# The attention sum of a graph layer: the next group's values weighed ahead of this group's one-hots

## The reference, cut to what matters

```python
q = (feat @ Wq.T + bq).reshape(n, H, HD)          # H = 8 heads of HD = 32
k = (feat @ Wk.T + bk).reshape(n, H, HD)
v = (feat @ Wv.T + bv).reshape(n, H, HD)
score = jnp.einsum('ehd,ehd->eh', q[edge_dst], k[edge_src])
score = jnp.clip(score / math.sqrt(HD), -10.0, 10.0)
...
ex = jnp.exp(score - smax[edge_dst])
den = jax.ops.segment_sum(ex, edge_dst, num_segments=n)
alpha = ex / den[edge_dst]
wv = jax.ops.segment_sum(alpha[:, :, None] * v[edge_src], edge_dst, num_segments=n).reshape(n, C)
```

## Time and profile before

| what | value |
|---|---|
| median of 3 runs | 4137.75 us (4130.2 to 4140.1) |
| the profiled execution's own time | 4135.46 us |
| its span (first to last instruction) | 4133.7 us |
| busy over the span: PE, DVE, ACT, POOL | 63%, 53%, 30%, 32% |
| attention sum, first product to last gather's landing | 2444 to 3240 us |

### The profile page before, as it was taken

How to read it: one execution, slowest core, us unless ns; L and a number is a source line. 1 busy time by engine, 2 the same in 40 slices (tenths; PEclk the granted TensorE clock), 3 DMA queues, 4 the chain that set the end, 5 groups by cost and what they waited for, 6 DMA issues and landing times. The chain is left out here.

```text
span 4133.7 us, 66642 instructions
## 1 busy us (share of the span) xinstructions
PE 2615.2 (63%) x17072; PEld 2109.2 (51%) x17073; DVE 2172.5 (53%) x4422; ACT 1260.5 (30%) x2441; POOL 1312.0 (32%) x996
## 2 busy tenths in 40 slices
PE   3513334437587799975654426666766487699993
PEld 2413333324276577753444325445545466589983
DVE  5623323231555488883347736666666655544443
ACT  0200000003244155551477512222222244244440
POOL 0038888842000000000001136667767500510015
PEclk9955555557688699987777658999888778799996
DMA  2036566730000000002000046666665100356643
GB/s 116 23 93 161 144 170 159 193 86 6 0 21 0 15 15 15 15 8 100 14 1 0 0 120 159 159 163 168 168 165 161 54 21 0 126 177 231 232 162 85
DMA packets 263746, 383.33 MB, mean 93 GB/s; under 512 B 122411, under 2 KB 189607, under 8 KB 258810
## 3 DMA queue, kind: packets, MB, share of 16 engines
q0 software_dynamic: 156960, 171.31, 16.8%
q1 hardware_dynamic: 93850, 199.08, 14.5%
q10 hardware_dynamic: 12864, 12.06, 1.0%
HBM read 318.81 MB, written 62.55 MB: 92 GB/s over the span
## 5 line engine op out<-in xcount | busy, mean ns | idle before, releaser
L1685 POOL DMA_INDIRECT as_gkv<-gather_kv,as_index x415 | 565.7, 1363 | 280.5 <-DVE as_index L1836 170.5
L745 POOL DMA_INDIRECT ms_got<-gather,ms_index x400 | 505.9, 1265 | 128.6 <-issue 109.3
L812 PE MATMUL ms_total<-ms_got,ms_hot 125*125 125x256 f16 x1040 | 231.7, 411 | 382.8 <-DMA ms_got<-gather,ms_index 292.9
L812 PEld LDWEIGHTS ms_total<-ms_got,ms_hot 125*125 x1040 | 203.6, 219 | 411.1 <-issue 411.1
L1806 PE MATMUL as_total<-as_gkv,as_hot 125*125 125x264 f32 x1040 | 280.0, 420 | 76.1 <-DVE as_summed L552 66.1
L2093 POOL MEMSET bm_fx<- 128x128 f32 x1 | 0.2, 204 | 1012.9 <-POOLq L114 1012.9
L1806 PEld LDWEIGHTS as_total<-as_gkv,as_hot 125*125 125x125 f32 x1040 | 201.2, 202 | 127.6 <-issue 91.4
L1479 ACT ACTIVATE ex_h<-ex_up,ex_now 128x313 f32<-128x313 f32 (+1 forms) x320 | 195.8, 612 | 197.6 <-PE ex_up L457 190.4
L2749 DVE CAST moe_hidden<-moe_h 128x256 f16<-128x256 f32 (+1 forms) x336 | 107.3, 319 | 206.2 <-ACT moe_h L2696 206.2
L1818 DVE TENSOR_TENSOR z_flat<-as_picked,as_gkv 125x1280 f32<-125x1280 f32 x81 | 120.4, 1487 | 176.7 <-DMA as_gkv<-gather_kv,as_index 130.2
L2696 ACT ACTIVATE moe_h<-moe_up,moe_w 128x256 f32<-128x256 f32 (+1 forms) x336 | 163.2, 486 | 140.3 <-PE moe_up L457 95.4
(11 more groups left out here) (431 smaller groups left out, 5859.1 us busy)
## 6 DMA issues: line engine op xcount, KB each, us to landing
moe_w<-wsplit SPq DMA_DIRECT2D x34, 2052.0 KB
as_dsts<-in_dst SPq DMA_DIRECT2D x83, 305.2 KB
wsplit<-ms_split SPq DMA_DIRECT2D x36, 512.0 KB, 4.3
pairs<-z_flat SPq DMA_DIRECT2D x4, 2048.0 KB, 21.5
ms_raw<-in_L_ffn_W1p SPq DMA_DIRECT2D x16, 512.0 KB, 6.9
ms_raw<-in_L_ffn_W2p SPq DMA_DIRECT2D x16, 512.0 KB, 9.2
moe_rows<-pairs SPq DMA_DIRECT2D x32, 256.0 KB
results<-moe_made SPq DMA_DIRECT2D x32, 256.0 KB, 8.2
```

Source lines behind the costliest of these rows:

```text
L745: pool.indirect_dma_start(out=got[:, s, j, :], out_offset=None, in_=m.gather0, in_offset=bass.IndirectOffsetOnAxis(ap=index[:, s, j:j + 1] ...
L812: ins = pe.matmul(total[:, visit % RING, 0:C], hot[:, visit % RING, j, :], got[:, s, j, p * C:(p + 1) * C], start=(j + p == 0), stop=(j + ...
L1685: pool.indirect_dma_start(out=gkv[:, s, j, 0:2 * C], out_offset=None, in_=m.gather_kv, in_offset=bass.IndirectOffsetOnAxis(ap=index[:, s, ...
```

## The change

In each of the four bodies, `weigh(n + 1)` moves from behind the loop of visits to the place between `next_index` and that loop. No instruction is added, removed or changed in shape, and no semaphore has another count.

```diff
                         next_index(n + SLOTS - 1, (s - 1) % SLOTS)
+                        weigh(n + 1, (s + 1) % SLOTS)
                         with dve.Fori(0, count) as k:
...
                             adder.add(visit, tile)
-                        weigh(n + 1, (s + 1) % SLOTS)
                 v.leave(G // SLOTS)
```

## The result

The changed kernel takes 4176.19 us, the median of 4 runs (4168.31 to 4177.7); the kernel before, run beside it, 4138.93 (4130.2 to 4141.86). The ratio is 1.009, 95% interval 1.007 to 1.011: **about 37 us slower**. That is 18 us beyond the upper end of the range. The profiled execution took 4177.7 us, 42.2 more than the one of before, with a span of 4176.0.

What follows compares the result with a forecast made beforehand. It took the bound to be a ring: a double body plus a two-body gather round. Double bodies +4.8, clock −2 and gathers −2 summed to +0.8 us, giving a forecast of 4138.5 us, range 4120 to 4158.

Steps and rivals of the forecast that it cites:

- The one-hots come later: On DVE, the one-hots start 1.50 us behind the index copy instead of 0.76, which is 0.74 later.
- Double bodies: Bodies with two visits: +0.1 us each, +0.5 at a trip's end, as the sequencer's table reading comes into the open; +4.8 us.
- Rival C: Double bodies take the whole 0.74 us delay, nothing won back behind the second visit: +18 us, 4156; chance 10%.
- The gathers' issue: POOL's gathers, held by DVE instructions with two SBUF inputs: 1.01 us a round instead of 1.08, −0.1 each, −2 in all.
- Rival D: Multiplication and one-hots back to back hold a round's first and fifth gathers 0.8 us longer: +38 us, 4176; chance 5%.
- Rival A: DVE's loop is the bound, so the covered idle ahead of the one-hots counts: −36 us, 4102; chance 5%.
- The lap: Stage's repeating unit: a double body plus a two-body gather round of 18.2 us from its end; shorter single bodies buy nothing.
- TensorE's clock: PE's first sums in double bodies, starting later, leave part of the low-clock stretch behind: −2 us, bounds −5 to +5.
- where the stretch ends when it did: Clock assumption: with the low-clock stretch's end fixed, a sum 0.74 us later leaves up to 0.37 us of it behind.
- the gathers' landing: Gather start to landing, called worst known: a shifted transfer of destinations could move it half a us either way, ±12 us.
- rival E: The gathers land later, mirror of a rival with sooner landings: +19 us, 4157; chance 7%.
- The signs: Checks in DVE's waits: waits for gathers grow by some 20 us; the wait for the first sum falls some us under 80.4.

Runs made afterwards that it cites:

- e9: Kernel before, with the wait for the last sum and the index copy moved between product and sum by head in each body: 4081.16 us, ratio 0.9873.
- e5: Kernel before, plus two matmuls of zeros into an unused bank between PE's picks and sum in every body: 4146.76 us, ratio 1.0011.
- e6: Changed kernel, plus two matmuls of zeros into an unused bank between PE's picks and sum: 4152.81 us, ratio 1.0029 to the kernel before.
- e1: Kernel before, with the transfers of destinations cut to 5 of 125 partitions from the third group on: 4103.43 us, ratio 0.9905.
- e2: Changed kernel, with the transfers of destinations cut to 5 of 125 partitions from the third group on: 4115.78 us, ratio 0.9931 to the kernel before.
- e3: Kernel before, with each full transfer of destinations issued later, waiting also for the next body's product: 4143.83 us, ratio 1.0002.
- e4: Changed kernel, with each full transfer of destinations issued later, waiting also for the next body's product: 4156.56 us, ratio 1.0037 to the kernel before.
- e8: Changed kernel, with destinations' transfers cut to 5 of 125 partitions and two matmuls of zeros between picks and sum: 4099.99 us, ratio 0.9904 to the kernel before.
- e7: Kernel before, with two memsets into an unused bank behind the index copy, delaying the one-hots without the move: 4177.45 us, ratio 1.008.

## Why the prediction was wrong

**Right.** *The one-hots come later*: 1.52 for 1.50 behind the index. *Double bodies*, the sequencer's part: behind the second one-hots the sequencer reads the table and reaches its last wait at 3058.9,

```profile
L523 DVEq TENSOR_LOAD <-group_table x1: 311/311/311, 3058.2 to 3058.2; - x1
```

```profile
L1817 DVEq EVENT_SEMAPHORE  x1: 21/21/21, 3058.9 to 3058.9; - x1
```

1.6 behind one-hots of 3057.28 (forecast 1.7), and the product starts 1.70 behind them (1.85). Where TensorE had its full clock through the body, a double body that is the first or second of its trip is 10.62 to 10.64 us long after and was 10.73: 0.1 shorter, not 0.1 longer. In the third place it is 10.84 (10.71 to 10.74 before), and in the last 11.15 to 11.16 (10.66 in two of four before), 0.5 longer as forecast for a trip's end. On average over all 24 bodies the one-hots' 0.74 costs 0.12 us, since 0.62 comes back behind the second ones: +3 in all, where +4.8 was forecast. Rival C, for which the product had to stay 2.53 behind, falls. *The gathers' issue*: the first gather of a round, the second and the one that meets the next body's multiplication,

```profile
3063.52 1.58 POOL L1685 DMA_INDIRECT as_gkv<-gather_kv,as_index  x1 [5.25 <-DVE as_index L1836]
3065.40 1.21 POOL L1685 DMA_INDIRECT as_gkv<-gather_kv,as_index  x1 [0.30 <-issue]
...
3069.97 1.69 POOL L1685 DMA_INDIRECT as_gkv<-gather_kv,as_index  x1 [0.30 <-issue]
```

took 1.58, 1.21 and 1.69; 1.57 and 1.21 were forecast for the first two, and for the last 1.21 + 0.65, 0.17 too much. The issue of the five took 8.03 us on average, 8.12 before: −0.09, and −0.1 was forecast. **Rival D had the number of the result, 4176, and is refuted all the same**: the first gathers of the 24 rounds took 1.57 to 1.59 us, nowhere near 2.2. The Trainium skill (SBUF — State Buffer, SBUF: two separate sides) infers that a two-input multiplication leaves descriptor generation alone; as in the earlier trace rows, the 1.58 us contradict it. Rival A falls, since the gather waits took up all that the single bodies lost, and more. *The lap*: held by e9.

**Wrong, first term: TensorE's clock.** I took −2 with −5 to +5 as bounds. The step that failed is "where the stretch ends when it did": I moved the sum 0.74 us along a stretch of low clock whose end I held fixed, or moved by as much. I did not ask what fills the 0.74. In most bodies of before there was no gap to fill, since the sum followed the picks; now PE pauses 0.77 there, right after the long pause of the gather wait. The stretch of low clock at the double body was 3.4 or 6.8 us long in 23 of the 24 laps of before; now it is 10.2 or 13.7 in 16 of them. The first sum grew from 3.06 to 3.64 on average, +0.58 × 24 = +14, which is what the wait for it shows (80.4 to 94.4). The other part of the body's +0.90 is ahead of the one-hots, which start 5.12 into the body where it was 4.19: +0.93, and not +0.74, since in four bodies (3, 22, 51, 70) the index itself waited for PE's last sum, +4.9 us in all; behind the second one-hots 0.62 comes back. With the +14 that is some +19 for TensorE's part; the fill gives back 23, a part of which it would give in the order of before as well, against a delay. Sign and size were both wrong. The pause has its row in the waits: PE's wait that the profile puts to the addition L552, right behind the one-hots for which PE waits, went from 66.1 us in 60 waits to 97.5 in 78. The Trainium skill (TensorE: Matmul & The Clock Gate, A second HAM failure mode) tells of a kernel whose clock goes up and down because TensorE idles for a moment between groups of matmuls; by e5 and e6 the trace agrees with it.

**Wrong, second term: the gathers' landing.** I had named the transfer of destinations as the thing that could be shifted, and bounded it at half a us either way, ±12 us. The landing rose by 1.18 us, × 24 = +28; with the issue's −0.09 that is the +1.09 of the two bodies. That is rival E with half as much again, to which I gave 7% and 19 us. The bound was half a us, taken without a row. The rows for the sign were there: single bodies of 6.75 us and of over 7.2 in the same trace had landings 2 us apart, and the change makes nearly all of them short. For the size they were not enough: by them it would have been some +10 us, and +18 if every lap had collided. So shorter single bodies, which by the lap "buy nothing", are not free: they place the transfer.

**The signs.** The waits for gathers grew by 54 us and not by 20, the rest being the second term. The wait for the first sum grew, where it was to fall, by the first. (The count of waits over 2.8 in the forecast is 14, not 13, which moves its bound by 0.4 us.)

The sum, put right from the lengths: +3 for the double bodies' own part, +19 for TensorE's and +26 for the rounds of the gather is +48, where the stage grew by 44.6; between the profiled executions it was 42.2 and between the medians 37.3. By the experiments, each edit compared in both orders, the loss falls from 37.3 to 12.4 (e1, e2), 12.7 (e3, e4) and 6 (e5, e6): 25 us for the landing and 31 for the matmuls, together more than there is. So both causes are shown, and how the loss divides between them is known only roughly. In e8 against e1, the move without the two, no loss is left, as the rest of the sum said.

**What stays open.** Why the landing is 8.61 us in one lap and 5.40 in another with the transfer at the same place, and why laps with the transfer at that place land 0.8 us later on average than they did before, I can't tell. Nor did I try a transfer issued earlier than before.

## What to carry to other kernels

A step that feeds TensorE and comes some tenths of a us later is not priced by its delay alone: see whether it opens a pause between two blocks of matmuls behind a long wait, and try a filler matmul in it, in the old order as well as in the new: the filler shortened the sums in both, and only the two together tell the clock's share. In a ring that is bound by a gather, shortening the bodies that wait moves the other transfers against it; look in the trace of before for laps that already have the new spacing. Their landing gives the sign; here it gave only a part of the size. And a rival whose number fits is not thereby the cause: D fitted the result, and the rows of its own mechanism refuted it.

## What the runs showed of the hardware

- A pause of 0.77 us on TensorE between two blocks, behind a wait of 8.32 us, went with a granted clock of 0.50 for 10.8 us (3046.0 to 3056.8). Two matmuls of 0.5 us each (e6) took the mean first sum from 3.64 to 2.71 us; in the order of before, mostly without the pause, the same two (e5) took it from 3.06 to 2.65.
- Laps in which a broadcast of 305.2 KB on SP's queue is issued within the fifth gather's issue had landings of 7.58 us on average in the kernel after and 6.77 in the kernel before, the others 5.06 and 5.03. With 5 of its 125 rows (e2) the mean over all laps is 4.57.
- A gather that starts while DVE works on two inputs in SBUF is held until that instruction is nearly over (1.58 and 1.69 us for 1.21; 2.53 in e7, where it starts with a multiplication of 1.49), but no longer when another such instruction follows directly behind it on DVE.
- Register, table and semaphore work of DVE's sequencer, 0.59 us a body where it stood open, vanished behind a multiplication of 1.49 us, and came back as 0.49 us (15.5 in 24 waits) where that multiplication had hidden it before.
